# Cross attention of block one: value products in three visits of four key tiles, over a ring of eight exponentials

## The reference, cut to what matters

```python
B, NQ, NK, D, H, DH = 32, 56, 1500, 128, 16, 8
h = _ln(x)
q = (h @ Wq + bq).reshape(Bx, Nx, H, D)
kv = (context @ Wkv + bkv).reshape(Bx, Mx, 2, H, D)
k, v = (kv[:, :, 0], kv[:, :, 1])
a = _sdpa(q, k, v).reshape(Bx, Nx, C)     # softmax(q k^T * scale) v, head by head
x = x + (a @ Woc + boc)
```

## Time and profile before

| | |
|---|---|
| median of three runs | 2256.37 us (2253.45 to 2263.25) |
| the profiled execution's own time | 2254.44 us |
| its span, first to last instruction | 2252.8 us |
| mean granted TensorE clock | 0.922 |
| PE busy | 1891.0 us, 84% |
| DVE busy | 1589.7 us, 71% |
| ACT busy | 1311.7 us, 58% |
| POOL busy | 1016.0 us, 45% |
| pieces' maxima on DVE (L1247) | 672, 429.0 us |
| exponentials on ACT (L1195) | 384, 349.4 us |
| value products on PE (L1158) | 6144 matmuls, 173.8 us |

### The profile page before, as it was taken

How to read it: one execution, slowest core, us unless ns; L and a number is a source line. 1 busy time by engine, 2 the same in 40 slices (tenths; PEclk the granted TensorE clock), 3 DMA queues, 4 the chain that set the end, 5 groups by cost and what they waited for, 6 DMA issues and landing times. The chain is left out here.

```text
span 2252.8 us, 57534 instructions
## 1 busy us (share of the span) xinstructions
PE 1891.0 (84%) x19877; PEld 1279.7 (57%) x19877; DVE 1589.7 (71%) x2772; ACT 1311.7 (58%) x2335; POOL 1016.0 (45%) x1183
## 2 busy tenths in 40 slices
PE   4888666689999999999978888445899999999988
PEld 3887334256666676666643455232566666666653
DVE  4899577666666666666632233796599999999984
ACT  2555233357666666676633343432688888888853
POOL 2333063345545445455300000461688888888840
PEclk7999898799999999999978899656899999999999
DMA  7776100133333333233205995000111111111100
GB/s 193 249 243 232 33 1 0 48 83 90 96 89 89 88 87 98 82 89 95 62 1 162 263 292 158 0 0 17 53 43 41 41 41 41 41 41 41 41 1 17
DMA packets 64288, 190.38 MB, mean 85 GB/s; under 512 B 19886, under 2 KB 27295, under 8 KB 64223
## 3 DMA queue, kind: packets, MB, share of 16 engines
q1 hardware_dynamic: 59614, 164.95, 26.3%
q0 software_dynamic: 4608, 24.58, 2.8%
HBM read 127.13 MB, written 25.49 MB: 68 GB/s over the span
## 5 line engine op out<-in xcount | busy, mean ns | idle before, releaser
L1247 DVE TENSOR_REDUCE c_part<-c_mxp 128x1 f32<-128x500 f32 x672 | 429.0, 678 | 211.5 <-PE c_mxp L1127 211.3
L1195 ACT ACTIVATE c_e<-c_stp 125x896 f32<-125x896 f32 x384 | 349.4, 917 | 167.5 <-PE c_stp L1141 166.1
L1890 ACT ACTIVATE c_e<-c_sp,alpha 128x750 f32<-128x750 f32 x448 | 392.2, 887 | 78.8 <-PE c_sp L1835 77.5
L1127 PE MATMUL c_mxp<-c_kh,c_qb 128*128 128x500 f16 x672 | 254.5, 381 | 7.1 <-DVE c_part L1247 3.7
L1926 DVE TENSOR_SCALAR c_ph<-c_e,c_inv 128x1500 f16<-128x1500 f32 x224 | 260.4, 1162 | 0.1
L1912 DVE TENSOR_SCALAR c_pt<-c_tp 125x768 bf16<-125x768 f16 x448 | 243.3, 546 | 1.2 <-PE c_tp L1848 0.4
L1848 PE MATMUL c_tp<-ident_h,c_ph 128*128 128x128 f16 x2688 | 224.1, 220 | 22.3 <-DVE c_pt L1912 21.8
L1848 PEld LDWEIGHTS c_tp<-ident_h,c_ph 128*128 128x128 f16 x2688 | 177.7, 98 | 106.6 <-DVE c_pt L1912 58.3
L1835 PE MATMUL c_sp<-c_ki,c_qb 128*128 128x375 bf16 x896 | 218.7, 326 | 12.2 <-ACT c_e L1890 11.7
L1141 PE MATMUL c_stp<-c_qs,c_ks 103*128 103x224 f16 x1536 | 210.2, 259 | 2.5 <-ACT c_e L1195 2.5
L1141 PEld LDWEIGHTS c_stp<-c_qs,c_ks 103*128 103x128 f16 x1536 | 147.1, 98 | 72.0 <-issue 20.3
(11 more groups left out here) (277 smaller groups left out, 3597.3 us busy)
## 6 DMA issues: line engine op xcount, KB each, us to landing
c_ct<-ctx_turned SPq DMA_DIRECT2D x64, 750.0 KB
ctx_turned<-l_ct POOLq DMA_DIRECT2D x32, 750.0 KB, 4.2
c_ks<-c_kh SPq DMA_DIRECT2D x256, 93.8 KB
f_ct<-ctx_turned SPq DMA_DIRECT2D x32, 750.0 KB
l_cn<-in_ctx SPq DMA_DIRECT2D x32, 672.0 KB
f_cn<-in_ctx SPq DMA_DIRECT2D x32, 672.0 KB
c_ks<-c_kl SPq DMA_DIRECT2D x128, 93.8 KB
l_cn<-in_ctx SPq DMA_DIRECT2D x32, 78.0 KB
```

Source lines behind the costliest of these rows:

```text
L1127: pe.matmul(mxp[:, (PIECES * p + s) % 2, 0:500], qh[p][:, 128 * (s // 3):128 * (s // 3) + 128], kh[p][:, 500 * (s % 3):500 * (s % 3) + 500 ...
L1195: act.activation(e[:, j % (2 * GROUP), :].rearrange("p (a c) -> p a c", a=2), stp[0:KP, 2 * (j % 2):2 * (j % 2) + 2, 0:448], ACT.Exp, scal ...
L1247: dve.reduce_max(part[:, s // 3, s % 3:s % 3 + 1], mxp[:, (PIECES * p + s) % 2, 0:500], axis=AX.X).then_inc(piece_max, 1)
L1890: act.activation(e[t % E_BUFFERS][:, HALF * h:HALF * h + HALF] .rearrange("p (k c) -> p k c", k=2), sp_[:, 2 * h:2 * h + 2, 0:375], ACT.Ex ...
```

## The change

GROUP becomes 4, so that a batch has three visits of four tiles, and the ring has eight places. Since 12 is no multiple of 8, the place of a tile now depends on the batch's parity p: (12p + j) % 8. The same parity is handed to `exponentials`. The visits move: slots 7, 10, 1 and 4 become slots 8, 0 and 4. The order of everything else stays as it is.

```diff
-        GROUP = 3
+        GROUP = 4
...
-        WEIGH_AT = {7: (2, 0), 10: (2, 1), 1: (3, 2), 4: (3, 3)}
+        WEIGH_AT = {8: (2, 0), 0: (3, 1), 4: (3, 2)}
...
                             last = pe.matmul(pvp[q:q + 32, c:c + width], vx[p][:, j, g, :],
-                                             e[:, j % (2 * GROUP), NQ * h:NQ * h + width], start=(j == 0 and g < 4),
+                                             e[:, (NJ * p + j) % (2 * GROUP), NQ * h:NQ * h + width], start=(j == 0 and g < 4),
...
-                def exponentials(a, j, later):
+                def exponentials(a, p, j, later):
                     act.wait_ge(scored, NJ * a + j + 1)
                     if j >= 2 * GROUP or later:
                         act.wait_ge(weighed, NJ * a + j + 1 - 2 * GROUP)
-                    act.activation(e[:, j % (2 * GROUP), :].rearrange("p (a c) -> p a c", a=2),
+                    act.activation(e[:, (NJ * p + j) % (2 * GROUP), :].rearrange("p (a c) -> p a c", a=2),
...
                         if j >= SCORE_AT and live(2):
-                            exponentials(n - 2, j - SCORE_AT, live(3))
+                            exponentials(n - 2, p, j - SCORE_AT, live(3))
                         if j < SCORE_AT and live(3):
-                            exponentials(n - 3, NJ + j - SCORE_AT, True)
+                            exponentials(n - 3, 1 - p, NJ + j - SCORE_AT, True)
```

## The result

| | before | after |
|---|---|---|
| median | 2254.91 us (2247.63 to 2263.25, 4 runs) | 2287.01 us (2285.96 to 2287.82, 4 runs) |
| ratio | | 1.013, 95% interval 1.0108 to 1.0151: slower |
| profiled execution | 2254.44 us | 2286.72 us |
| span | 2252.8 us | 2285.1 us |

The change makes the kernel 1.3% slower (the quotient of the two medians, 1.014, lies inside the interval). The page of the changed kernel shows little of it: TensorE's share is the same 84%, and VectorE's fell from 71% to 69%.

What follows compares the result with a forecast made beforehand. The prediction took PE as the bound, with DVE's maxima late in bare slots. Terms 10.9 + 10.9 + 10.2 + 1.2 + 1.8 - 4.0 = +31.0 us on 2254.4, plus 1.9 for the median, gave 2287.4 us, range 2274 to 2297.

Steps and rivals of the forecast that it cites:

- three bare slots: Slots 7, 10 and 1, left without visit or projection, make PE wait for DVE's maxima: +10.9, +10.9 and +10.2 us.
- turning behind piece 20: In slot 11 the turning of the maxima comes 1.41 us behind piece 20, 0.04 more, 31 times: +1.2 us.
- visits and their entries: 128 visits become 96; 31 fewer up to the drain, at 0.13 us each, save 4.0 us.
- What bounds the stage: PE is the bound, busy 20.71 of 21.31 us a batch; its every gain or standstill goes into the time.
- The price of a bare slot: PE stands 0.35 us in each slot without visit or projection, or 0.34 behind a visit.
- The price of a visit: Each visit costs 0.13 us of its own: 0.09 for entering and 0.04 for leaving.
- The double slot: Slot 8, with a visit and a value projection, starves DVE for 1.7 and 0.9 us but costs nothing by itself.
- The turn of the loop: Every second step has 0.3 us more, ahead of slot 0, where it was before.
- The drain: After the last turning, visits of four tiles make the end come at +20.4 us instead of +18.6: +1.8 us.
- waits for ACT: Rival: behind double slot 8, V of slot 9 waits 0.5 us more for ACT, adding 15 us: 2303 us; chance 0.04.
- the clock stayed at 1.00: Rival: new gaps in slots 10 and 11 lower PE's clock, about 1 us more a batch, 2318 us; chance 0.02.
- made up by other work: Rival: PE finds other work or DVE catches up sooner, so the time is 2254 us; chance 0.07.

Runs made afterwards that it cites:

- e3: The changed kernel with each maximum taken over 250 of a piece's 500 columns: 2248.81 us, ratio 0.9947.
- e12: The changed kernel with each maximum taken over 125 of a piece's 500 columns: 2235.16 us, ratio 0.9884.
- e4: The changed kernel with the second value projection moved from slot 8 to slot 7: 2269.25 us, ratio 1.0054.
- e7: The changed kernel with its visits of four tiles in slots 7, 11 and 3 and keys in 1, 2, 5: 2248.64 us, ratio 0.9968.
- e9: The kernel before with one of its four visits moved from slot 7 to slot 8: 2267.47 us, ratio 1.0038.
- e1: The kernel before with only the ring enlarged to eight, old visits kept: 2259.51 us, ratio 0.9997.
- e5: The kernel before with the turning of the maxima placed behind the score of slot 11: 2252.96 us, ratio 0.9978.
- e10: The kernel before with visits in 8, 11, 1, 5, keys in 2, 3, 4, values in 6, 7, 9, piece 20 behind its score: 2231.51 us, ratio 0.9871.

## Why the prediction was right

The forecast was 2287.4 us and the median is 2287.01. The terms, from the distances between starts in one batch:

| term, us a batch | predicted | measured |
|---|---|---|
| three bare slots | +1.04 | +1.03 (0.34, 0.34, 0.35) |
| turning behind piece 20 | +0.04 | +0.03 (1.40 instead of 1.37) |
| visits and their entries | -0.13 | -0.24 |
| projections | 0 | +0.14 |
| sum | +0.95 | +0.96 |

- *What bounds the stage.* Right: PE's list with its standstills sets the batch, and DVE's idle time at large says nothing about it. e3 and e12 show the cause: shorten the maxima and the loss goes, all but 3 us in e3 and all of it in e12. e4 and e7 show that the place of the visits decides, not their length.
- *The price of a bare slot*, taken from two places where the kernel before had one, held to 0.01 us in all three new places, and in e9 and e4 one at a time.
- *The price of a visit* was too small, 0.13 us where 0.23 is right. Four tiles take 709.58 - 707.91 = 1.67 us from the visit's start to the next piece, not 1.71, and three took 704.10 - 702.81 = 1.29. So the fourth tile costs 0.38 us (0.383 by the unrounded starts), some 24 ns for each of its 16 matmuls and not 26.1, and a visit has 1.29 - 3 * 0.383 = 0.14 us beyond its tiles, where I had 0.04 for leaving; the 0.09 of entering comes on top. My 26.1 ns was the distance over 36 matmuls, two tiles and a quarter from the visit's first start, and the starts are not evenly spaced: in the trace they come in fours, some 7 ns apart, with 0.15 us behind the first four, and 0.12 or 0.03 us behind the later ones. Three visits take 5.01 us where four took 5.16, and one entry of 0.09 is saved: the saving has the forecast sign and is small, but nearly twice what I had.
- *The double slot was not free.* I had asked what it does to DVE and to ACT, and not how long the projection itself takes behind a visit: 0.10 us more, which e9 repeats. The first key projection takes 0.04 more (711.56 to 712.44, 0.88), for a reason that I have not looked for. These two hide the error in the visits, which is luck.
- *The turn of the loop* gave a little back: the longer batches exceed the shorter ones by 0.16 to 0.21 us instead of 0.30. From the first turning to the last it is 1152.59 - 461.37 = 691.22 us instead of 1122.77 - 459.05 = 663.72: +27.5, where I had +29.2.
- *The drain* grew by 1.4 us, not 1.8. I had counted 0.42 us for each further tile, where it is 0.38; the rest of the difference I have not followed.
- The stage therefore gives +28.9 us, not +31.0. The two spans differ by 32.3: another 2.3 us lie ahead of the first turning and 1.1 behind the drain. Both vary where the code is the same: in the profiles of the kernel before, e1, e5 and e9 the first turning falls between 459.05 and 462.15 us, and in all profiles of this study the end of the kernel is 1104 to 1114 us behind the end of the drain. So the hit on the exact value is luck by some us; the stage's part was off by 2.1 us, 7%. The ratio of 1.013, 24 to 34 us by its interval, fits either number.
- *Rivals.* No matmul of the changed kernel waits for ACT in the steady state, the clock stayed at 1.00 with the new gaps, and no part of the standstills was made up by other work.

## What to carry to other kernels

When PE's order is written out by hand and a slower engine takes its results through two banks, the long pieces of other work between them are that engine's cover. Spread them so that no stretch without cover is longer than the banks can carry, and put one ahead of each point where PE waits for the end of a chain; in e10 this gave 1.3%, while fewer and longer visits in the wrong slots lost as much. Here the price of a place without cover could be read off in advance where the pipeline fills and drains, since some of the cover is missing there.

## What the runs showed of the hardware

- A maximum over 500, 250 and 125 columns of fp32 in PSUM took 0.678 to 0.679, 0.418 and 0.287 to 0.288 us by the medians: about 1.04 ns a column and 0.16 us for each instruction, by the differences.
- A piece, its maximum and the release of the bank made a chain of 1.14 to 1.16 us with 500 columns and 0.91 with 250. What a single bare slot costs is this chain less PE's own 0.80 us: with 250 columns two maxima need less than 0.80 of DVE, and yet the slot cost 0.10.
- Value products of 32 output columns, four side by side, took 0.38 us for a key tile of 16 matmuls. A visit had 0.23 us of its own beside that, 0.09 ahead of its first matmul and 0.14 from there to the next piece, with three tiles as with four.
